# A state-space layer on one core: the output products set between the two key products, the finish behind the near levels, and a ring bank planned as read 2.4 steps on

## The chip, the core and the metric

The kernel runs on one core of a Trainium2 chip. The core's engines run side by side, each through its own list of instructions in order: TensorE multiplies matrices (its results go to a memory of their own, PSUM), VectorE and ScalarE work on tiles in SBUF and PSUM, GpSimd on tiles in SBUF, and it also issues the gathers; SyncE issues the other transfers. They wait for one another by semaphores. The metric is the device time of one execution in microseconds, lower is better.

## What is computed

Six layers of a small model on 4 sequences of 1024 positions of width 128: an expert layer, a state-space layer, the same expert layer again, then a layer of low-rank experts, an attention layer and the low-rank experts again. The change is in the state-space layer alone. Cut to what matters of it:

```python
proj = x @ W_in                       # z, x_raw, B (R=2 keys), C, dt, lam, theta
x_raw = silu(x_raw)
Bm = rms(Bm) * B_norm_bias;  Cm = rms(Cm) * C_norm_bias
dt = clip(softplus(dt_raw + dt_bias), 0.0001, 0.5)
ang = -cumsum(mean(dt) * theta)
Cr, Br = rope(Cm, cos, sin), rope(Bm, cos, sin)
xg = (lam * dt) * xh;  xb = ((1 - lam) * dt * alpha) * x_prev
cum = cumsum(log_dA) in each chunk of 128;  dmat = exp(cum_l - cum_m) for m <= l
y_intra = (C_l . B_m) * dmat * xg  +  (C_l . Bprev_m) * dmat * xb
S_next = exp(cum_end) * S + (decayed B, x of the chunk)
y_inter = C_l . S * exp(cum_l)
y = rms((y_intra + y_inter) * silu(z));  x = x + y @ W_out
```

## The kernel before

The layer (function `ssm`) is one stage of the program; the stages follow one another on all engines. The 4096 positions are 32 chunks of 128, numbered n, eight to a sequence (a "batch" b) and four to a group g. The heads' work is done for all 32 heads at once.

**One chunk**, in the order in which its data pass:

- TensorE transposes the rotated keys and queries of the chunk (`turn`, L1266, L1268) into a bank of the ring, and ScalarE copies them out to `bct` (`copy_turned`, L1472).
- TensorE multiplies keys with queries (`dots`, L1286 to L1289), once for each of the two keys r. Below these are called r0 and r1. Between them stands a wait for r0's result to be written. Blocks near the diagonal are masked on VectorE (`near_levels`, L1704, tile `near`), the far ones copied on ScalarE (`far_levels`, L1479).
- VectorE makes the weighted inputs `X` (`weigh`, L1713), GpSimd two more of them (L1539).
- TensorE forms the chunk's contribution to the state (`next_state`, L1297) and the output in three parts (`levels`: a first block of L1307, a second one of L1307, L1332 and L1335, and the product with the state, L1339). The blocks wait until VectorE has scaled those of the chunk before.
- VectorE carries the state on (`states`: the decay L1731 and the sum L1736) and scales and sums the three parts (`scale`, L1750, L1757, L1761, tile `ysum`).
- GpSimd multiplies with the gate (`sum_up`, L1549, tile `u_out`); ScalarE takes its squares (`square`, L1488); TensorE transposes it (`turn_out`, L1347), ScalarE copies that to `uT` (L1495).
- TensorE forms the output product (`project_out`, L1355), and VectorE adds it to the residual and takes the statistics for the next normalization (`finish`, L1768 and L108).

Three chunks are in flight in this manner, and between their instructions stands the preparation of later groups: projections (L1209, L1216, L1225), decays and rotations (`coefficients`, L1234 to L1254 on TensorE, L1597 to L1680 on VectorE), and the gathers of the expert layer's outputs (L263, added by VectorE in L271).

**The order** on each engine is written as step times. A helper (`interleave`) sorts all pieces on an engine by start plus step: `yield 21` in `project_out(n)` means "at K[n] + 21", where K[n] grows by 12 from chunk to chunk. Nothing runs at these times: they only give the order. So `dots(n+3)`, with steps -14 and -13, stands at K[n] + 22 and K[n] + 23.

**The ring** is four PSUM banks that all of TensorE's other results share, strictly in turn. A planner (`Uses`) gives each use its place in the turn, by the step at which it is written and the step by which it is planned to be read; where the bank would not be free by then it moves the whole rest of that stream to a later step. A stream wrapped in `moving(...)` follows its own moves. `dots`, `near_levels` and `far_levels` are not such streams: they stand at fixed steps.

Of the kernel before, what the change touches and what calls it, by code (L numbers as in the profile page):

```python
# [17 lines left out]
TILES = BATCHES * TIME // P  # L18
# [1059 lines left out]
def ssm(core, tag, weights, combine):  # L1078
# [14 lines left out]
    with ExitStack() as ctx:  # L1093
# [3 lines left out]
        def sem(name):  # L1097
            return core.stage_sem(f"{tag}_{name}")
# [48 lines left out]
        K = [FIRST + PERIOD * n for n in range(TILES)]  # L1147
# [8 lines left out]
        streams = {}  # L1156
# [6 lines left out]
        for n in range(TILES):  # L1163
            streams["t", n] = K[n], [(("t", n), -18, -16)]
            if n % NT < NT - 1:
                streams["st", n] = K[n], [(("st", n), -0.6, 2.6)]
            streams["u", n] = K[n], [(("u", n), 17.5, 19.5)]
            streams["r", n] = K[n], [(("r", n), 21, 23.5)]
        uses = Uses([ring[:, i, :] for i in range(4)], [sem(f"full{i}") for i in range(4)], [sem(f"free{i}") for i in range(4)], streams)

        def moving(name, stream):
            return 0, uses.moving(name, stream)
# [28 lines left out]
        with nc.Block(no_gpsimd_drain=True) as block:  # L1201
            @block.tensor
            def _(pe):
# [67 lines left out]

                def dots(n):

                    yield -14
                    uses.wait_read(pe, ("t", n))
                    if n:
                        pe.wait_ge(S["near_ready"], n)
                        pe.wait_ge(S["far_ready"], n)
                    for r in range(R):
                        if r:  # L1280
                            yield -13
                            pe.wait_ge(S["s_done"], 2 * n + 1)
                        rows, o = slice(r * N, (r + 1) * N), ps_s[:, n % 2, r, :]
                        k, q = bct[rows, n % 2, 0, :], bct[rows, n % 2, 1, :]
                        for m in range(0, P, BLOCK):
                            t_.matmul(o[m:m + 32, 0:32], k[:, m:m + 32], q[:, m:m + 32], start=True, stop=True, skip_group_check=True)  # L1286
                        for m in (0, 64):
                            t_.matmul(o[m:m + 32, 32:64], k[:, m:m + 32], q[:, m + 32:m + 64], start=True, stop=True, skip_group_check=True)
                        ins = t_.matmul(o[0:64, 64:128], k[:, 0:64], q[:, 64:128], start=True, stop=True, skip_group_check=True)  # L1289
                        ins.then_inc(S["s_done"], 1)  # L1290
# [57 lines left out]
                    uses.written(ins, ("u", n))  # L1348

                def project_out(n):  # L1350
                    yield 21
                    uses.wait_read(pe, ("u", n))
                    ps = uses.take(pe, ("r", n))
                    for i in range(2):
                        ins = t_.matmul(ps[:, 0:D], uT[:, n % 2, i, :], wout[:, i, :], start=(i == 0), stop=(i == 1))  # L1355
                    uses.written(ins, ("r", n))

                interleave([(K[n], levels(n)) for n in range(TILES)] + [(K[n], dots(n)) for n in range(TILES)] +
                           [moving(("t", n), turn(n)) for n in range(TILES)] + [moving(("st", n), next_state(n)) for n in range(TILES) if n % NT < NT - 1] +
                           [moving(("u", n), turn_out(n)) for n in range(TILES)] + [moving(("r", n), project_out(n)) for n in range(TILES)] +  # L1360
# [4 lines left out]
            def _(act):  # L1365
# [106 lines left out]
                    uses.read(s_.copy(bct[:, n % 2].rearrange("p j t -> p (j t)"), ps[:, 0:2 * P]), ("t", n))  # L1472

                def far_levels(n):
                    yield -10.8
                    act.wait_ge(S["near_ready"], n + 1)
                    if n >= 2:
                        act.wait_ge(S["o_done"], 3 * (n - 1))
                    s_.copy(far[0:96, n % 2], ps_s[0:96, n % 2, :, BLOCK:]).then_inc(S["far_ready"], 1)  # L1479
# [87 lines left out]
            def _(dve):  # L1567
# [128 lines left out]
                    rotate(1)  # L1696

                def near_levels(n):
                    yield -12
                    dve.wait_ge(S["s_done"], 2 * n + 2)  # L1700
                    if n >= 2:
                        dve.wait_ge(S["o_done"], 3 * (n - 1))
                    shape = [P, 4, R, BLOCK]
                    v.tensor_tensor(near[:, n % 2], ps_s[:, n % 2, :, 0:BLOCK].unsqueeze(1).broadcast_to(shape),  # L1704
                                    masks[:].unsqueeze(2).broadcast_to(shape), ALU.mult).then_inc(S["near_ready"], 1)
# [55 lines left out]
                    v.tensor_tensor(ysum[:], Y6[:, 0], Y6[:, 1], ALU.add).then_inc(S["summed_up"], 1)  # L1761

                def finish(n):
                    yield 23.5, ("r", n)
                    ps = uses.wait(dve, ("r", n))
                    dve.wait_ge(S["urs_ready"], n + 1)
                    xt = core.x[:, n, :]
                    uses.read(v.scalar_tensor_tensor(xt, ps[:, 0:D], urs[:, n % 2:n % 2 + 1], xt, ALU.mult, ALU.add), ("r", n))  # L1768
                    uses.wait_read(dve, ("r", n))
                    dve.sem_inc(S["added"], 1)  # L1770
                    core.count(n)
# [700 lines left out]
```

## Time and profile before

| what | value |
|---|---|
| median of 3 runs | 1458.83 us (1457.34 to 1461.06) |
| the profiled execution | 1452.51 us, span of its instructions 1450.7 us |
| mean granted clock of TensorE in it | 0.856 |
| TensorE busy (matmul) | 1167.0 us, 80% |
| VectorE busy | 1117.8 us, 77% |
| ScalarE busy | 804.8 us, 55% |
| GpSimd busy | 658.4 us, 45% |

Busy time is the time in which an engine worked on an instruction, including the time in which the instruction itself was held up. An idle time is put down to the instruction that ended it (the releaser). The granted clock is a share of full speed: 1.00 is 2.4 GHz and 0.50 is 1.2 GHz. In the rows of an order of time, neighbouring instructions of one kind are merged, with their count.

### The profile page before, as it was taken

What the parts mean: (1) busy time and instruction counts of PE and PEld (TensorE: products, weight loads), DVE (VectorE), ACT (ScalarE), POOL (GpSimd) and SP (SyncE); (2) the same over time, 40 slices, a digit from 0 to 9 for tenths busy, and PEclk for the clock granted to TensorE, in tenths of its full rate; (3) what the DMA queues carried; (4) which work ended last, traced back from release to release, by engine and by line L of the source; (5) the groups of instructions that cost most, each with busy time, mean ns of one, the idle gap of its engine ahead of it and who ended that gap; (6) DMA issues with size and microseconds to landing.
All of it is one profiled execution on the core that took longest, in us unless ns stands there. A gap on an engine that the chain in (4) does not pass through costs nothing. (4 is left out here: it accounts for less than half of the span.)

```text
span 1450.7 us, 32990 instructions
## 1 busy us (share of the span) xinstructions
PE 1167.0 (80%) x11380; PEld 740.1 (51%) x11380; DVE 1117.8 (77%) x2557; ACT 804.8 (55%) x1477; POOL 658.4 (45%) x859
## 2 busy tenths in 40 slices
PE   7679963798988989898848995458987988898894
PEld 6369952455545545554627994343433544443333
DVE  6959973888888897899786996567868877876644
ACT  3768844445235325311347884127876677778781
POOL 2366633763674674356347663453333431521100
PEclk6779985698988889999658997558998999999996
DMA  8035340000000000000502332000000000000000
GB/s 284 13 91 174 90 61 21 22 9 2 23 9 2 20 12 1 2 2 1 173 26 75 91 89 51 15 15 10 7 23 5 17 26 1 16 8 9 1 16 8
DMA packets 55714, 55.09 MB, mean 38 GB/s; under 512 B 9882, under 2 KB 44484, under 8 KB 55556
## 3 DMA queue, kind: packets, MB, share of 16 engines
q1 hardware_dynamic: 46468, 34.37, 7.5%
q0 software_dynamic: 9088, 18.63, 6.0%
q8 instruction: 98, 1.61, 0.5%
q14 instruction: 60, 0.49, 0.1%
HBM read 32.26 MB, written 20.71 MB: 37 GB/s over the span
## 5 line engine op out<-in xcount | busy, mean ns | idle before, releaser
L2143 ACT ACTIVATE l_probs<-l_ps 128x1024 f32<-128x1024 f32 (+1 forms) x320 | 288.0, 946 | 100.1 <-PE l_ps L2029 98.2
L781 POOL DMA_INDIRECT ffn_yg<-y_rows,ffn_index x156 | 156.1, 1001 | 82.5 <-PE ffn_ps_t L796 39.6
L2048 PE MATMUL l_ps<-l_probs,l_vs 128*32 128x512 f32 (+3 forms) x1536 | 165.1, 519 | 27.3 <-DVE l_oTs L2376 15.8
L864 ACT ACTIVATE ffn_hT<-ffn_ps_h,experts_b1T,experts_scales 128x256 f32<-128x256 f32 x312 | 151.1, 563 | 30.6 <-PE ffn_ps_h L811 29.8
L263 POOL DMA_INDIRECT combine_og<-o_rows,combine_place x128 | 139.3, 1088 | 54.0 <-issue 31.5
L1307 PE MATMUL ssm_ps<-ssm_X,ssm_near 32*32 32x256 f32 x2048 | 138.2, 421 | 1.9 <-DVE ssm_Y L1750 1.9
L2367 DVE TENSOR_TENSOR l_probs<-l_probs,last_tri 128x256 f32<-128x256 f32 x256 | 101.8, 435 | 41.4 <-ACT l_probs L2143 39.9
L2029 PE MATMUL l_ps<-l_qkT 32*128 32x512 f16 (+3 forms) x768 | 109.7, 338 | 18.1 <-ACT l_probs L2143 16.0
L889 DVE SCALAR_TENSOR_TENSOR ffn_h<-ffn_hT,experts_scales,ffn_h 128x512 f16<-128x512 f32 x156 | 117.2, 751 | 5.5
L827 PE MATMUL ffn_ps_o<-experts_w,ffn_h 128*128 x624 | 113.0, 220 | 2.1 <-DVE ffn_h L889 2.0
L1549 POOL TENSOR_TENSOR ssm_u_out<-ssm_ysum,ssm_zx 128x256 f32<-128x256 f32 x32 | 69.0, 2157 | 99.4 <-DVE ssm_ysum L1761 99.3
L829 PE MATMUL ffn_ps_o<-experts_w,ffn_h 128*128 x624 | 111.1, 220 | 0.0
L830 PE MATMUL ffn_ps_o<-experts_w,ffn_h 128*128 x624 | 111.1, 220 | 0.0
L886 DVE TENSOR_SCALAR ffn_h<-ffn_hT,experts_scales 128x512 f16<-128x512 f32 x156 | 80.9, 519 | 30.3 <-ACT ffn_hT L864 27.2
L2029 PEld LDWEIGHTS l_ps<-l_qkT 32*128 32x128 f16 x768 | 29.6, 92 | 145.8 <-ACT l_probs L2143 103.8
L1307 PEld LDWEIGHTS ssm_ps<-ssm_X,ssm_near 32*32 32x32 f32 x2048 | 66.0, 117 | 70.5 <-issue 38.2
L2214 POOL COPY l_vs<-l_V 128x144 f32<-128x144 f32 (+1 forms) x32 | 13.5, 421 | 181.6 <-PE l_ps L2048 181.5
L1750 DVE TENSOR_TENSOR ssm_Y<-ssm_ps,ssm_outp 128x512 f32<-128x512 f32 x96 | 65.1, 686 | 38.1 <-PE ssm_ps L1335 19.0
L1713 DVE TENSOR_TENSOR ssm_X<-ssm_zx,ssm_xw 128x2560 f32<-128x2560 f32 x32 | 90.3, 2821 | 0.1
L1479 ACT COPY ssm_far<-ssm_ps 96x192 f32<-96x192 f32 x32 | 10.1, 315 | 144.6 <-DVE ssm_near L1704 144.6
L809 PE MATMUL ffn_ps_h<-ffn_ygT,experts_w 128*128 128x256 f16 x312 | 86.8, 278 | 3.5 <-ACT ffn_ygT L855 3.4
L271 DVE SCALAR_TENSOR_TENSOR x_res<-combine_og,combine_gates,x_res 128x128 f32<-128x128 f32 x128 | 53.8, 420 | 44.2 <-DMA combine_og<-o_rows,combine_place 40.5
(354 smaller groups left out, 2965.9 us busy)
## 6 DMA issues: line engine op xcount, KB each, us to landing
o_rows<-ffn_out_sb SPq DMA_DIRECT2D x78, 128.0 KB, 1.9
y_rows<-ffn_y SPq DMA_DIRECT2D x8, 512.0 KB, 4.9
kept_w<-experts_w SPq DMA_DIRECT2D x16, 256.0 KB
experts_w<-kept_w SPq DMA_DIRECT2D x16, 256.0 KB, 5.6
ffn_yg<-y_rows,ffn_index POOLq DMA_INDIRECT x156
x_res<-in_L_attn_x SPq DMA_DIRECT2D x4, 512.0 KB, 6.2
prep_raw<-in_L_ffn_W SPq DMA_DIRECT2D x1, 2048.0 KB, 10.7
prep_raw<-in_L_ffn_W SPq DMA_DIRECT2D x8, 256.0 KB, 5.5
```

What stands on the lines that cost most here:

```text
L263: self.core.nc.gpsimd.indirect_dma_start(self.og[:, tile % GRING, k], None, self.o_rows.ap(), bass.IndirectOffsetOnAxis(ap=self.place[:, k ...
L781: g_.indirect_dma_start(yg[:, i % RING, j].rearrange("p n d -> p (n d)"), None, w.y_rows.ap(), bass.IndirectOffsetOnAxis(ap=index[:, n:n + ...
L827: t.matmul(o, h16[:, i % 2, 0, c, rows], high, start=(c == 0 and j == 0), stop=False, skip_group_check=True)
L829: t.matmul(o, h16[:, i % 2, 0, c, rows], low, start=False, stop=False, skip_group_check=True)
L830: ins = t.matmul(o, h16[:, i % 2, 1, c, rows], high, start=False, stop=(c == HC - 1), skip_group_check=True)
L864: s.activation(hT[:, i % 2, c, :], ps_h[:, i % 2, c, :], ACT.Gelu, bias=w.b1T[:, bass.ds(e * HC + c, 1)], scale=SC[:, 6:7]).then_inc(h_rea ...
L889: v.scalar_tensor_tensor(h16[:, i % 2, 1, part], hT[:, i % 2, part], SC[:, 5:6], h16[:, i % 2, 0, part], ALU.mult, ALU.subtract).then_inc( ...
L1307: ins = t_.matmul(o[rows], near[rows, n % 2, k, r, :], weighed(n, x, r, rows), start=start, stop=stop, skip_group_check=True)
L2029: ins = t_.matmul(ps_s[w % 2][:, i, at:at + width], qkT[r, b % 2, hg, 1, kb * P:(kb + 1) * P], qkT[r, b % 2, hg, 0, q0:q0 + width], start= ...
L2048: ins = t_.matmul(ps_o[VP * h:VP * h + VP, q0 % H:q0 % H + width], vs[:, s % 2, kb, h, :], probs[:, n % PSLOTS, i, at:at + width], start=( ...
L2143: s_.activation(probs[:, w % PSLOTS, i:i + n, 0:width], ps_s[w % 2][:, i:i + n, 0:width], ACT.Exp, scale=SCALE / (UNIT * UNIT)).then_inc(S ...
L2367: v.tensor_tensor(p, p, tri[:].unsqueeze(1).broadcast_to([P, n, P]), ALU.mult).then_inc(S["m_done"], 1)
```

## The change

Three numbers of steps are changed, and one list is added:

- `project_out(n)` stands at 22.6 instead of 21, that is between r0 (22) and r1 (23) of `dots(n+3)`.
- Its bank is planned as written at 22.6 and read at 25 (2.4 later), before at 21 and 23.5; `finish(n)` stands at 25 instead of 23.5, that is behind `near_levels(n+3)` (24) and the decay of chunk n+2 (24.5).
- `LATER[n]` is how far the planner has moved the transpose of chunk n, less 1.5. `dots`, `near_levels` and `far_levels` are put later by it. It is 1.6 for n = 6, 14 and 22, and 0 for all others.

```diff
-            streams["r", n] = K[n], [(("r", n), 21, 23.5)]
+            streams["r", n] = K[n], [(("r", n), 22.6, 25)]
         uses = Uses([ring[:, i, :] for i in range(4)], [sem(f"full{i}") for i in range(4)], [sem(f"free{i}") for i in range(4)], streams)
+
+        LATER = [max(0, uses.at(("t", n), -16) - (K[n] - 16) - 1.5) for n in range(TILES)]
...
                 def dots(n):
 
-                    yield -14
+                    yield -14 + LATER[n]
...
                         if r:
-                            yield -13
+                            yield -13 + LATER[n]
...
                 def project_out(n):
-                    yield 21
+                    yield 22.6
...
                 def far_levels(n):
-                    yield -10.8
+                    yield -10.8 + LATER[n]
...
                 def near_levels(n):
-                    yield -12
+                    yield -12 + LATER[n]
...
                 def finish(n):
-                    yield 23.5, ("r", n)
+                    yield 25, ("r", n)
```

Two lines are added, so all lines behind them are 2 higher in the changed kernel (L1731 is L1733 there).

On VectorE, in the last batch, the order of one chunk was

```order
L1761 TENSOR_TENSOR ssm_ysum<-ssm_Y 128x256
L1713 TENSOR_TENSOR ssm_X<-ssm_zx,ssm_xw 128x2560
L1768 SCALAR_TENSOR_TENSOR x_res<-ssm_ring,ssm_urs,x_res 128x128
L108 BN_STATS ln_stats<-x_res 128x6
L1704 TENSOR_TENSOR ssm_near<-ssm_ps,states_masks 128x256
L1731 TENSOR_TENSOR ssm_state<-ssm_state,ssm_outp 128x256
L1736 TENSOR_TENSOR ssm_state<-ssm_state,ssm_ring 128x256
L1750 TENSOR_TENSOR ssm_Y<-ssm_ps,ssm_outp 128x512 x2
```

and is in the changed kernel

```order
L1763 TENSOR_TENSOR ssm_ysum<-ssm_Y 128x256
L1715 TENSOR_TENSOR ssm_X<-ssm_zx,ssm_xw 128x2560
L1706 TENSOR_TENSOR ssm_near<-ssm_ps,states_masks 128x256
L1733 TENSOR_TENSOR ssm_state<-ssm_state,ssm_outp 128x256
L1770 SCALAR_TENSOR_TENSOR x_res<-ssm_ring,ssm_urs,x_res 128x128
L108 BN_STATS ln_stats<-x_res 128x6
L1738 TENSOR_TENSOR ssm_state<-ssm_state,ssm_ring 128x256
L1752 TENSOR_TENSOR ssm_Y<-ssm_ps,ssm_outp 128x512 x2
```

The finish and its statistics stand behind near and the decay. GpSimd's order does not change.

On TensorE, where the ring's plan is moved (chunk 6 in the stretch around 354 us), the order was

```order
L1355 MATMUL ssm_ring<-states_wout,ssm_uT 128x128 x2
L1266 MATMUL ssm_ring<-ident,ssm_rot 128x128
L1268 MATMUL ssm_ring<-ident,ssm_rot 64x128 x2
L1286 MATMUL ssm_ps<-ssm_bct 32x32 x4
L1288 MATMUL ssm_ps<-ssm_bct 32x32 x2
L1289 MATMUL ssm_ps<-ssm_bct 64x64
L1286 MATMUL ssm_ps<-ssm_bct 32x32 x4
L1288 MATMUL ssm_ps<-ssm_bct 32x32 x2
L1289 MATMUL ssm_ps<-ssm_bct 64x64
L1297 MATMUL ssm_ring<-ssm_X,ssm_rot 64x256 x2
L1307 MATMUL ssm_ps<-ssm_X,ssm_near 32x256 x28
```

and is

```order
L1268 MATMUL ssm_ring<-ident,ssm_rot 128x128
L1270 MATMUL ssm_ring<-ident,ssm_rot 64x128 x2
L1357 MATMUL ssm_ring<-states_wout,ssm_uT 128x128 x2
L1299 MATMUL ssm_ring<-ssm_X,ssm_rot 64x256 x2
L1288 MATMUL ssm_ps<-ssm_bct 32x32 x4
L1290 MATMUL ssm_ps<-ssm_bct 32x32 x2
L1291 MATMUL ssm_ps<-ssm_bct 64x64
L1309 MATMUL ssm_ps<-ssm_X,ssm_near 32x256 x24
L1288 MATMUL ssm_ps<-ssm_bct 32x32 x4
L1290 MATMUL ssm_ps<-ssm_bct 32x32 x2
L1291 MATMUL ssm_ps<-ssm_bct 64x64
L1309 MATMUL ssm_ps<-ssm_X,ssm_near 32x256 x4
```

The transpose of chunk 6 stands ahead of the output product of chunk 3 and takes its turn in the ring, r0 comes behind the state product of chunk 5, and r1 behind the first block of chunk 5's level products. VectorE's near of chunk 6 now stands behind its finish there, and ScalarE's far copy behind the scaling of twelve keys (L1437) and a square.

In the plain chunks TensorE's order changes from (output product, r0, r1) to (r0, output product, r1); in some of them a piece of the preparation stands between.

## Rows read from the trace of the kernel before

**Rows 1.** Busy time by stretch: length, PE, PEld, DVE, ACT, POOL, clock, DMA share, GB/s.

```profile
628.00:705.00 77.00, 65.51 (x824) 36.42 (x823) 66.97 (x93) 10.71 (x40) 41.20 (x34) 0.90 0.01 2
```

**Rows 2.** VectorE in order of time, last batch: start, duration, instruction, [idle before].

```profile
645.61 0.34 DVE L1768 SCALAR_TENSOR_TENSOR x_res<-ssm_ring,ssm_urs,x_res 128x128 f32<-128x128 f32 x1
...
646.30 0.41 DVE L1704 TENSOR_TENSOR ssm_near<-ssm_ps,states_masks 128x256 f32<-128x256 f32 x1
646.63 1.82 DVE L1731 TENSOR_TENSOR ssm_state<-ssm_state,ssm_outp 128x256 f32<-128x256 f32 x1
648.48 0.42 DVE L1736 TENSOR_TENSOR ssm_state<-ssm_state,ssm_ring 128x256 f32<-128x256 f32 x1
649.12 1.29 DVE L1750 TENSOR_TENSOR ssm_Y<-ssm_ps,ssm_outp 128x512 f32<-128x512 f32 x2 [0.21 <-DVE ssm_state L1736]
```

**Rows 3.** The decays on VectorE, last batch: count, ns shortest/median/longest, first and last start.

```profile
L1731 DVE TENSOR_TENSOR ssm_state<-ssm_state,ssm_outp x6: 1812/1815/1819, 636.7 to 686.5; 128x256 f32<-128x256 f32 x6
```

**Rows 4.** GpSimd in order of time, same chunk as rows 2.

```profile
643.03 3.24 POOL L1549 TENSOR_TENSOR ssm_u_out<-ssm_ysum,ssm_zx 128x256 f32<-128x256 f32 x1 [3.86 <-DVE ssm_ysum L1761]
646.23 1.93 POOL L1539 TENSOR_TENSOR ssm_X<-ssm_zx,ssm_xw 128x1024 f32<-128x1024 f32 x1
```

**Rows 5.** VectorE and GpSimd in order of time, near 296 us and 543 us.

```profile
296.29 0.99 DVE L1731 TENSOR_TENSOR ssm_state<-ssm_state,ssm_outp 128x256 f32<-128x256 f32 x1
...
296.88 0.97 POOL L1549 TENSOR_TENSOR ssm_u_out<-ssm_ysum,ssm_zx 128x256 f32<-128x256 f32 x1
...
543.00 0.41 DVE L1731 TENSOR_TENSOR ssm_state<-ssm_state,ssm_outp 128x256 f32<-128x256 f32 x1
...
542.33 0.73 POOL L1549 TENSOR_TENSOR ssm_u_out<-ssm_ysum,ssm_zx 128x256 f32<-128x256 f32 x1
543.01 2.20 POOL L1539 TENSOR_TENSOR ssm_X<-ssm_zx,ssm_xw 128x1024 f32<-128x1024 f32 x1
```

**Rows 6.** TensorE in order of time, same chunk; the last row is ScalarE.

```profile
646.33 0.44 PE L1347 MATMUL ssm_ring<-ident,ssm_u_out 128*128 128x128 f32 x2 [0.62 <-POOL ssm_u_out L1549]
...
647.78 0.71 PE L1355 MATMUL ssm_ring<-states_wout,ssm_uT 128*128 128x128 f32 x4 [0.54 <-ACT ssm_uT L1495]
648.42 0.27 PE L1286 MATMUL ssm_ps<-ssm_bct 64*32 64x32 f32 x8
...
649.06 0.27 PE L1286 MATMUL ssm_ps<-ssm_bct 64*32 64x32 f32 x8
...
649.56 0.65 PE L1297 MATMUL ssm_ring<-ssm_X,ssm_rot 128*64 128x256 f32 x4
...
647.63 0.37 ACT L1472 COPY ssm_bct<-ssm_ring 128x256 f32<-128x256 f32 x1
```

**Rows 7.** TensorE in order of time, around 354 us; the last two rows are VectorE.

```profile
353.75 0.68 PE L1355 MATMUL ssm_ring<-states_wout,ssm_uT 128*128 128x128 f32 x4 [3.16 <-DVE ssm_xw L1641]
...
355.39 0.33 PE L1286 MATMUL ssm_ps<-ssm_bct 64*32 64x32 f32 x8 [0.47 <-ACT ssm_bct L1472]
...
358.09 4.36 PE L1307 MATMUL ssm_ps<-ssm_X,ssm_near 32*32 32x256 f32 x44
362.09 0.40 PE L1332 MATMUL ssm_ps<-ssm_X,ssm_far 32*32 32x256 f32 x2
...
359.79 0.41 DVE L1736 TENSOR_TENSOR ssm_state<-ssm_state,ssm_ring 128x256 f32<-128x256 f32 x1
...
363.52 0.69 DVE L1750 TENSOR_TENSOR ssm_Y<-ssm_ps,ssm_outp 128x512 f32<-128x512 f32 x1
```

**Rows 8.** VectorE in order of time, the chunk after rows 7.

```profile
372.84 0.42 DVE L1704 TENSOR_TENSOR ssm_near<-ssm_ps,states_masks 128x256 f32<-128x256 f32 x1 [1.21 <-PE ssm_ps L1289]
...
376.18 0.69 DVE L1750 TENSOR_TENSOR ssm_Y<-ssm_ps,ssm_outp 128x512 f32<-128x512 f32 x1 [2.12 <-PE ssm_ps L1307]
```

**Rows 9.** TensorE's idle time before line 1286, whole stage: releaser, us, times.

```profile
  PE ssm_ps L1289: 5.0, 23
```

**Rows 10.** As rows 1, for three microseconds of the last batch.

```profile
660.00:663.00 3.00, 3.00 (x24) 1.13 (x28) 2.90 (x6) 0.00 (x0) 0.05 (x1) 0.50 0.03 5
```

## The prediction

> **What bounds the kernel now.** I read the page first: the changed code is one stage, the state-space layer, which runs from about 281 to 705 us. The next stage starts only when this one is over on all engines, so what the stage loses or gains goes to the end at full size. Then the busy time by stretch [rows 1]: in the last part of the stage, 628 to 705 us, no engine is full: TensorE is busy 65.5 of 77 us, VectorE 67.0, at a mean granted clock of 0.90. So the bound changes from place to place, and must be read from the order of time. Two places matter.
>
> In the last batch (chunks 25 to 30) VectorE has no idle time but the 0.21 us behind its own state sum [rows 2]. The decays of the state, one per chunk, start from 636.7 to 686.5 us [rows 3]: five periods in 49.8 us, 9.96 us each. VectorE sets that pace. TensorE waits twice in a period, 0.62 us for GpSimd's u_out and 0.54 us for the copy uT [rows 6], so it needs 9.96 - 0.62 - 0.54 = 8.80 us.
>
> Elsewhere in the stage TensorE is mostly ahead of VectorE in the queue for time: VectorE stands 1.21 us for the key products and 2.12 us for the first level products of the chunk [rows 8]. There a reordering on VectorE costs or gives nothing, and one on TensorE counts.
>
> **The change, part by part.**
>
> *Finish behind near levels and decay, on VectorE (all chunks).* No instruction is added. The decay (L1731) has two inputs in SBUF. In the last batch it takes 1.81 us, six times of six [rows 3]; at 543 us, with nothing in front of it, 0.41 us [rows 5]. What it waits for is GpSimd: the product L1539 starts at 646.23 and runs 1.93 us, to 648.16, and the decay that started at 646.63 ends at 648.45 [rows 2, 4], 0.29 us after it. Now follow the new order from 645.61, where the finish started and near can start: near has its input long before (its products were done a chunk ago) and takes 0.33 us from start to next start, so the decay is ready at 645.94. GpSimd is then still in u_out, which ends at 643.03 + 3.24 = 646.27 [rows 4]. The decay waits 0.33 us for that, runs 0.42 us, and is over at about 646.7. Finish and its statistics take 646.30 - 645.61 = 0.69 us [rows 2], so the state sum starts at about 647.4 instead of 648.48: 1.07 us saved per chunk. Six chunks give 6.4 us.
>
> That needs the decay to get in between two GpSimd instructions that stand behind one another. Rows speak for it: the decay of 296.29 took 0.99 us, so it ended at 297.28, and the u_out that started at 296.88 took 0.97 us instead of 0.73 [rows 5]; and at 543.00 the decay took its 0.41 us where u_out ended at 543.06, and L1539, started at 543.01, took 2.20 us instead of 1.93. In both the waiting decay went first and GpSimd's next instruction paid about 0.25 us. L1539 is then 0.4 us later in each chunk; it is used a chunk later, and GpSimd's share is low (41 of 77 us, rows 1), so this costs nothing. The Trainium skill, "SBUF — State Buffer", section "Who interferes with whom", says that a VectorE instruction with two SBUF inputs and a GpSimd instruction that reads SBUF exclude each other for the whole instruction, and that the order of issue decides. The trace agrees (1.81 against 0.41 us). The page does not say who is next when one waits and the other has a second instruction behind; by it alone the gain could be 0 or 1.07 us a chunk.
>
> How much of the 6.4 us TensorE lets through: the new VectorE period is 9.96 - 1.07 = 8.9 us, TensorE's need 8.80, so the gain just fits. I take off 0.4 us for the six chunks together, since TensorE's order changes too (next part). Last batch: -6.0 us.
>
> *Output product between the two key products, on TensorE.* Before: wait for uT, output product, products r0, a wait of 0.2 us for r0 to be written, r1. After: wait for bct, r0, output product, r1. The short wait is filled: 5.0 us in 23 places over the stage [rows 9]. Against it, where TensorE stands idle for uT, the output product used to run while ScalarE made bct (uT released it at 647.78, bct was ready at 647.63 + 0.37 = 648.0 [rows 6]); now TensorE stands until 648.0. From 648.0: r0 0.44, output product 0.64, r1 about 0.5, so the next state product at 649.6 against 649.56. Nothing gained where it waits for uT. But uT itself stands on ScalarE behind the far copy, which waits for near, and near is 0.69 us earlier: in the last batch that makes bct about 0.3 us earlier, which is what holds TensorE's need at 8.8. Where TensorE is the bound and does not wait for uT, the 0.2 us is real; I count four such chunks, -0.8 us. Bounds: 0 and -5.0 us (all of rows 9).
>
> In the other chunks with a wait for key products on VectorE, near starts no earlier, and finish, once in that wait, now comes after: the state sum is 0.69 us later. VectorE then stands 2.12 us for TensorE anyway [rows 8], which hides it: 0 (bounds 0 and +0.7 in each of six such chunks).
>
> *Shifted ring plan (chunks 6, 14, 22).* The transpose of these chunks moves ahead of the output product of the chunk three back, the state product ahead of r0, and r1 behind the first 24 level products. From 353.75 to 362.09 TensorE needs 8.34 us, of which 0.47 us is a wait for bct [rows 7] and about 0.15, rounded down from rows 9, the wait for r0. Both are filled: the second block of level products, at 362.09, starts 0.6 us earlier, three times: -1.8 us. Price on VectorE: near now waits for r1, which ends just before that second block, at about 361.5. Behind it stand near itself (0.33) and, from the state sum to the first scaling, 363.52 - 359.79 = 3.73 us [rows 7]: the first scaling comes at 365.5, 2.0 us later. In the next chunk VectorE has 1.21 + 2.12 us of idle time [rows 8], so it is hidden. Bounds per place: -1.1 and +2.0 us.
>
> Sum: -6.0 - 0.8 - 1.8 = **-8.6 us**. The profiled execution took 1452.51 us (span 1450.7), so its like after the change would take 1443.9. It lies 6.3 us under the median of the runs shown, 1458.83; on the median the same sum gives **1450.2 us**.
>
> **The rivals.**
>
> *GpSimd keeps the port (slower).* If L1539, issued right at the end of u_out, takes the port before the waiting decay, the decay ends at 648.45 as before and finish with its statistics comes behind it: +0.69 us in each of six chunks, +4.1 us. It decides at one point: whether the decay, ready 0.33 us before u_out ends, goes first. With the other two terms at nothing this gives 1463.0; with them 1460.4. For it: L1539 seems to start (646.23) even before u_out's end. Against it: both cases of rows 5.
>
> *TensorE takes over.* The need of 8.80 us holds at the full clock. In the last batch there are 3 us and more at half the clock [rows 10]; if it stays so, TensorE, not VectorE, is late after each such stretch, and half of the 6.4 us is lost: about -5, 1453.8 us. Such a stretch follows idle time of TensorE, of which there would be less.
>
> *The clock helps too.* If that stretch goes away because of less waiting, TensorE gets about 3 us back and other waits for uT shrink as near comes earlier: 1445.
>
> *The shifted places cost.* If the 2.0 us on VectorE is not hidden in three places, +6.0 instead of -1.8: 1458.0.
>
> *Nothing moves.* If the decay still lands in L1539 because all engines shift together: 1458.
>
> **How the numbers follow.** Forecast 0.50 (own range 1447 to 1453); clock helps 0.08; TensorE takes over 0.14, half of it beyond 0.3%; shifted places 0.10; port kept 0.12, of which 0.10 slower than 0.3%, as other decays would be held too; nothing 0.06. 0.3% is 4.4 us, about what a measurement of this kernel can tell from no change. Faster: 0.50 + 0.08 + 0.08 = 0.66; same: 0.06 + 0.10 + 0.02 + 0.06 = 0.24; slower 0.10. Range: 1445 to 1460, which leaves out most of the port case and the best end.
>
> **What would show it.** Right: in the last batch the decays take 0.75 us or so instead of 1.81, L1539 takes over 2 us, and their starts are 8.9 us apart. Wrong: decays still at 1.8 us with the statistics behind them, or TensorE without waits there. In the shifted chunks VectorE should stand about 1.7 us before near, and the next level products should come 0.6 us earlier. What would make the prediction wrong as a whole: half-clock stretches at other places, each worth 2 to 3 us of TensorE's time.

## The result: 0.8% faster, and the profile after

| what | before | changed |
|---|---|---|
| median, 4 runs each | 1459.38 us (1457.34 to 1461.06) | 1445.15 us (1442.62 to 1452.10) |
| the profiled execution | 1452.51 us | 1452.10 us |
| its span | 1450.7 us | 1450.3 us |
| mean granted clock | 0.856 | 0.860 |
| next stage begins at | 705.10 us | 698.45 us |

The ratio is 0.9918, 95% interval 0.9897 to 0.9940: 12 us less by the ratio and 14.2 by the two medians, where 8.6 were forecast. The two profiled executions look equal, and that is chance: that of before lies 5 us under the lowest of its other runs, that of the changed kernel is the highest of its four. Inside the trace the gain is plain until well into the last stage. VectorE in order of time (start, duration, instruction, idle before), changed kernel, first row the beginning of the next stage, second row an addition in the attention layer:

```profile
698.45 0.21 DVE L119 TENSOR_TENSOR ln_tmp<-ln_stats 128x32 f32<-128x32 f32 x1 [0.39 <-PEq L1203]
...
1143.67 0.68 DVE L2397 SCALAR_TENSOR_TENSOR x_res<-l_ps,x_res 128x512 f32<-128x512 f32 x1
```

and of before:

```profile
705.10 0.21 DVE L119 TENSOR_TENSOR ln_tmp<-ln_stats 128x32 f32<-128x32 f32 x1 [0.39 <-PEq L1201]
...
1150.22 0.68 DVE L2395 SCALAR_TENSOR_TENSOR x_res<-l_ps,x_res 128x512 f32<-128x512 f32 x1
```

6.65 us ahead at the stage's end, 6.55 still at 1144 us. Then it is lost, in code that the change doesn't touch, and the last column but two (granted clock) says where. Busy time by stretch (length, PE, PEld, DVE, ACT, POOL, clock, DMA share, GB/s), changed kernel:

```profile
1144.00:1228.00 84.00, 74.69 (x614) 36.52 (x615) 64.96 (x185) 58.69 (x76) 23.39 (x47) 0.92 0.05 14
...
1266.00:1343.00 77.00, 70.43 (x575) 31.99 (x576) 53.34 (x143) 58.01 (x73) 13.51 (x31) 0.89 0.03 8
```

and the same pieces of work before:

```profile
1150.00:1231.00 81.00, 71.02 (x608) 34.20 (x608) 64.74 (x185) 58.71 (x76) 23.92 (x48) 0.96 0.05 14
...
1270.00:1343.00 73.00, 66.70 (x590) 30.32 (x592) 53.24 (x143) 58.84 (x74) 12.97 (x30) 0.98 0.03 9
```

In the first pair the changed kernel needs 84 us at a clock of 0.92 for what took 81 at 0.96. At 1266 us it is 3.4 us ahead, at 1343 it is 1.2 us behind. It is the trace of before that is unusual: what comes behind the state-space stage takes 745.6 us in it, and 750.1 to 757.2 us in the nine other traces of the table below. A second profile of the same kernel (`after_again`, below) ended its stage at 691.37 us and its span at 1441.8. So one pair of profiles can't give the total here; the medians do, and the traces tell the mechanism within the stage.

**The last batch** did what was forecast. VectorE and GpSimd in order of time, changed kernel, to be held against [rows 2, 4]:

```profile
664.37 0.42 DVE L1706 TENSOR_TENSOR ssm_near<-ssm_ps,states_masks 128x256 f32<-128x256 f32 x1
664.70 0.61 DVE L1733 TENSOR_TENSOR ssm_state<-ssm_state,ssm_outp 128x256 f32<-128x256 f32 x1
665.35 0.35 DVE L1770 SCALAR_TENSOR_TENSOR x_res<-ssm_ring,ssm_urs,x_res 128x128 f32<-128x128 f32 x1
665.85 0.29 DVE L108 BATCH_NORM_STATS2 ln_stats<-x_res 128x6 f32<-128x128 f32 x1
666.06 0.40 DVE L1738 TENSOR_TENSOR ssm_state<-ssm_state,ssm_ring 128x256 f32<-128x256 f32 x1
...
661.79 3.24 POOL L1551 TENSOR_TENSOR ssm_u_out<-ssm_ysum,ssm_zx 128x256 f32<-128x256 f32 x1 [2.55 <-DVE ssm_ysum L1763]
665.00 2.11 POOL L1541 TENSOR_TENSOR ssm_X<-ssm_zx,ssm_xw 128x1024 f32<-128x1024 f32 x1
```

The decay is ready at 664.70, waits for u_out's end (661.79 + 3.24 = 665.03), runs, and is over at 665.31. GpSimd's product behind it takes 2.11 us, 0.18 more than before: it paid the wait. From near's start to the state sum VectorE needs 1.69 us; before it needed 648.48 - 645.61 = 2.87 us for the same four instructions [rows 2]. The decays as a group (count, ns shortest/median/longest, first and last start), as in [rows 3]:

```profile
L1733 DVE TENSOR_TENSOR ssm_state<-ssm_state,ssm_outp x6: 614/619/621, 637.4 to 682.2; 128x256 f32<-128x256 f32 x6
```

The last four periods are 8.77 us (the first 9.77, with a half-clock stretch from 631 to 638 us just ahead of it), where all were 9.96. VectorE still sets the pace: it has no idle time but the 0.22 us behind its state sum. The half-clock stretch that before has from 659 us on is gone, as one rival had it, but it is not what gives the gain: before's periods are 9.96 with it and without it.

**TensorE's waits** in the stage moved. The product's and the key products' groups, changed kernel (busy us, mean ns | idle us ahead, by releaser):

```profile
L1357 PE MATMUL ssm_ring<-states_wout,ssm_uT 128*128 128x128 f32 x128 | 24.0, 314 | 1.4 <-ACT ssm_uT L1497 1.4
...
L1288 PE MATMUL ssm_ps<-ssm_bct 64*32 64x32 f32 x480 | 16.4, 208 | 14.1 <-ACT ssm_bct L1474 14.1
```

before:

```profile
L1355 PE MATMUL ssm_ring<-states_wout,ssm_uT 128*128 128x128 f32 x128 | 24.2, 317 | 26.6 <-ACT ssm_uT L1495 17.2 <-DVE ssm_xw L1641 9.5
...
L1286 PE MATMUL ssm_ps<-ssm_bct 64*32 64x32 f32 x480 | 17.0, 215 | 2.7 <-ACT ssm_bct L1472 1.4
```

The 5.0 us between r0 and r1 [rows 9] are gone, and the wait for uT (17.2 us) has become one for bct (14.1 us); with the 1.4 us of the other kind on each side it is 23.6 us before and 15.5 after. Other waits of TensorE in the stage grew meanwhile: those for the layer's input y (`ssm_y`), for the state and for the scaling together take 22.4 us where they took 14.8. Whether the move is worth anything the experiments have to say.

**A shifted place**, chunk 6. TensorE and VectorE in order of time, changed kernel, to be held against [rows 7]:

```profile
355.98 0.30 PE L1268 MATMUL ssm_ring<-ident,ssm_rot 128*128 128x128 f32 x1 [3.16 <-DVE ssm_xw L1643]
...
357.81 0.27 PE L1288 MATMUL ssm_ps<-ssm_bct 64*32 64x32 f32 x8
...
358.46 4.24 PE L1309 MATMUL ssm_ps<-ssm_X,ssm_near 32*32 32x256 f32 x48
362.63 0.26 PE L1288 MATMUL ssm_ps<-ssm_bct 64*32 64x32 f32 x8
...
363.25 0.42 DVE L1706 TENSOR_TENSOR ssm_near<-ssm_ps,states_masks 128x256 f32<-128x256 f32 x1 [1.48 <-PE ssm_ps L1291]
```

No wait for bct is left, near stands 1.48 us for r1 (I had said 1.7), and from the end of the wait to the second block TensorE takes 7.19 us where it took 8.34: 1.15 less, not 0.6. In the two other places it takes 7.10 and 7.07.

### The profile page after: what moved, and what is told of

It reads as the page before. It is cut to its first block and busy times, and to the rows that moved or that the text cites. A ratio compares the mean times of both kernels' runs of the same rounds, so it can differ in the third digit from the quotient of the medians.

```text
span 1450.3 us, 32972 instructions
## 1 busy us (share of the span) xinstructions
PE 1165.1 (80%) x11380; PEld 740.9 (51%) x11380; DVE 1116.0 (77%) x2557; ACT 806.5 (56%) x1477; POOL 660.2 (46%) x859
## 5 line engine op out<-in xcount | busy, mean ns | idle before, releaser
L263 POOL DMA_INDIRECT combine_og<-o_rows,combine_place x128 | 143.8, 1124 | 54.8 <-issue 32.9
L1309 PE MATMUL ssm_ps<-ssm_X,ssm_near 32*32 32x256 f32 x2048 | 132.3, 406 | 4.6 <-DVE ssm_Y L1752 4.6
L809 PE MATMUL ffn_ps_h<-ffn_ygT,experts_w 128*128 128x256 f16 x312 | 86.9, 279 | 3.4 <-ACT ffn_ygT L855 3.3
L811 PE MATMUL ffn_ps_h<-ffn_ygT,experts_w 128*128 128x256 f16 x312 | 86.9, 279 | 0.0
L810 PE MATMUL ffn_ps_h<-ffn_ygT,experts_w 128*128 128x256 f16 x312 | 86.9, 279 | 0.0
```

What stands on the lines that cost most here:

```text
L263: self.core.nc.gpsimd.indirect_dma_start(self.og[:, tile % GRING, k], None, self.o_rows.ap(), bass.IndirectOffsetOnAxis(ap=self.place[:, k ...
L1309: ins = t_.matmul(o[rows], near[rows, n % 2, k, r, :], weighed(n, x, r, rows), start=start, stop=stop, skip_group_check=True)
```

## The experiments

Each kernel is compared with runs of the kernel before on the same chip, in between its own. For the stage itself I use one number from each trace, its length from the first near (chunk 0) to the beginning of the next stage, and three parts of it:

| kernel | what it has of the change | ratio to before (95%) | stage, us | the three places, us | last batch, five sums, us |
|---|---|---|---|---|---|
| before | nothing | | 429.1 | 8.34, 8.52, 8.26 | 50.15 |
| finish_alone | finish | 0.9990 (0.9969 to 1.0011) | 424.7 | 8.41, 8.51, 8.53 | 43.86 |
| product_alone | output product | 1.0067 (1.0047 to 1.0088) | 434.6 | 8.61, 8.73, 8.72 | 50.15 |
| shift_alone | shift | 0.9995 (0.9974 to 1.0016) | 423.3 | 6.79, 6.83, 6.83 | 50.16 |
| no_product | finish, shift | 0.9886 (0.9858 to 0.9914) | 414.0 | 6.79, 6.79, 6.79 | 43.84 |
| no_finish | product, shift | 0.9972 (0.9951 to 0.9992) | 423.4 | 7.05, 7.04, 7.04 | 50.15 |
| no_shift | finish, product | 0.9973 (0.9954 to 0.9993) | 421.5 | 8.29, 8.68, 8.73 | 43.86 |
| changed, first profile | all | 0.9918 (0.9897 to 0.9940) | 422.5 | 7.19, 7.10, 7.07 | 43.85 |
| after_again | all | 0.9924 (0.9901 to 0.9948) | 416.1 | 7.05, 7.04, 7.04 | 43.84 |
| decay_first | decay moved, no part of the change | 0.9956 (0.9932 to 0.9979) | 424.1 | 8.21, 8.57, 8.50 | 45.45 |

"Places" is the time from the end of TensorE's wait for xw (3.15 or 3.16 us in every one) to the start of its second block of level products, for chunks 6, 14 and 22. "Five sums" is the time between the starts of the tile ysum of chunks 25 and 30, read from the order of time. The stage column holds one execution each; the changed kernel's two differ by 6.4 us, so it is a guide and no verdict. The last two columns repeat to 0.02 us and, but for the clock (below), to 0.1 to 0.3 us.

### One part at a time

`finish_alone`, against the changed kernel:

```diff
-        LATER = [max(0, uses.at(("t", n), -16) - (K[n] - 16) - 1.5) for n in range(TILES)]
+        LATER = [0 for n in range(TILES)]
-            streams["r", n] = K[n], [(("r", n), 22.6, 25)]
+            streams["r", n] = K[n], [(("r", n), 21, 25)]
-                    yield 22.6
+                    yield 21
```

> Only the finish is moved behind the near levels and the decay (step 25); the output product stays at 21 and nothing is shifted. Port theory: GpSimd's second product of X no longer holds the decay, so in the last batch the decays take about 0.62 us (1.81 before) and start 8.8 us apart (9.96 before): about -7 us between the decays of chunks 25 and 30, all of the change's gain there. In the part of the stage before 628 us the finish ahead of the state sum costs what it costs in the changed kernel, 0 to +1 us. Total about 1450. Rival (the order on TensorE is what made it possible): the starts stay over 9.4 us apart, because TensorE then waits for uT in front of the key products, and less than half of the gain comes.

The decays took 615 to 620 ns, and the five sums 43.86 us where before has 50.15: the whole gain of the last batch, with TensorE's order as it was. The rival (TensorE's order makes it possible) falls. The ratio of 0.9990 is no measurable gain in the total, although the stage is 4.4 us shorter in its trace.

`product_alone`: the same with 22.6 kept, its bank planned as read at 23.5, and `finish` back at 23.5.

> Only the output product is moved between the two key products (step 22.6); the finish stays at 23.5 ahead of near, nothing is shifted. Port theory: the decays of the last batch stay at 1.81 us and 9.96 us apart, nothing is gained there; in the chunks before, 0 to -0.8 us from the filled wait between r0 and r1. Total within 2 us of before. Rival (TensorE's order carries the gain): the last batch's starts come under 9.5 us apart.

Its decays stay at 1.82 us and the five sums at 50.15, as the port theory says. But it is slower than before by 0.67%, which neither theory had. Its trace shows a wait of VectorE's finish that was 1.0 us in 3 times before (us, times, longest):

```profile
DVE x_res L1770 <- PE ssm_ring L1357: 7.6, 8, 1.9
```

and, behind the batch boundaries, additions of the gathered rows held by GpSimd, VectorE then GpSimd near 414 us:

```profile
414.50 3.42 DVE L271 SCALAR_TENSOR_TENSOR x_res<-combine_og,combine_gates,x_res 128x128 f32<-128x128 f32 x2
...
415.45 1.93 POOL L1541 TENSOR_TENSOR ssm_X<-ssm_zx,ssm_xw 128x1024 f32<-128x1024 f32 x1
```

Such a pair takes 0.73 us when it is free. In this trace pairs near 297, 384, 414, 503 and 533 us are held; before has those near 297, 384 and 500. Of the stage's 5.5 us more in this trace, 3.0 come between the sums of chunks 8 and 9, at 414 us; that the held pair there costs nothing, and the clock does, is shown under `after_again`. What the other 2.5 us and the rest of the 0.67% come from isn't shown.

`shift_alone`: `LATER` as in the changed kernel, all other numbers as before.

> Only the list of shifts is added (key products, near and far copy of chunks 6, 14 and 22 are 1.6 steps later). My prediction: second block of level products 0.6 us earlier at three places, -1.8 us up to 628 us, last batch as before (9.96 us apart). Rival (it costs VectorE 2 us per place, not hidden): up to +6 us by 628 us.

The places take 6.8 us in place of 8.3 to 8.5, 1.4 to 1.7 less in each; between the tile ysum of chunks 4 and 7, 12 and 15, 20 and 23 the stage is 1.7, 2.0 and 1.8 us shorter. So the sign and the hiding on VectorE were right and the size was three times too small. The total shows nothing (0.9995).

`after_again` is the changed kernel.

> The changed kernel again, for the spread. If the state-space stage runs alike in every execution, its end lies again at 698.4 us, within 0.5 us, and the executions' differences (1442.6 to 1452.1 us) come from the attention layer, behind 1100 us. Rival: the stage's end itself wanders by some microseconds with the half-clock stretches.

The rival is right: the stage ended at 691.37 us, 7.1 us earlier than in the first profile. Of that 0.6 us lie ahead of the stage, 1.4 us come in chunk 1, where only the first profile has a half-clock stretch (290 to 293 us), 1.0 us in chunks 4 and 5, and 3.3 us between the sums of chunks 8 and 9. At this last step a pair is held as in product_alone. First profile, VectorE, GpSimd and TensorE:

```profile
415.72 3.04 DVE L271 SCALAR_TENSOR_TENSOR x_res<-combine_og,combine_gates,x_res 128x128 f32<-128x128 f32 x1
...
416.67 1.93 POOL L1541 TENSOR_TENSOR ssm_X<-ssm_zx,ssm_xw 128x1024 f32<-128x1024 f32 x1
...
417.13 3.92 PE L1309 MATMUL ssm_ps<-ssm_X,ssm_near 32*32 32x256 f32 x48
```

`after_again`, the same additions:

```profile
411.60 0.74 DVE L271 SCALAR_TENSOR_TENSOR x_res<-combine_og,combine_gates,x_res 128x128 f32<-128x128 f32 x2
```

In the one it was ready 0.3 us before GpSimd's u_out and was held through that and the product of X; in the other it was over before u_out began. Whether it meets them differs from execution to execution. But the hold is not what costs the 3.3 us. In decay_first (below) the same addition is held even longer, and its sum of chunk 9 comes 0.4 us later than in before, as that of chunk 8 does:

```profile
414.81 3.17 DVE L271 SCALAR_TENSOR_TENSOR x_res<-combine_og,combine_gates,x_res 128x128 f32<-128x128 f32 x1
...
414.68 2.79 PE L1307 MATMUL ssm_ps<-ssm_X,ssm_near 32*32 32x256 f32 x48
```

What differs is the clock. The first profile and product_alone have half clock from 402 to 419 us, decay_first only to 412.3, and `after_again` to 409. The first block of level products takes 3.92 and 4.35 us in the first two, 2.79 in the others, and VectorE then waits for TensorE. So the two executions of the changed kernel differ here by the clock.

### One part taken away

`no_product`, against the changed kernel (the output product back at 21, ahead of both key products):

```diff
-            streams["r", n] = K[n], [(("r", n), 22.6, 25)]
+            streams["r", n] = K[n], [(("r", n), 21, 25)]
-                    yield 22.6
+                    yield 21
```

> The changed kernel with the output product back ahead of both key products (step 21, planned read at 25). If the parts only added up (finish alone -3.0, shift alone -2.7 us in the medians so far) it would take 1452 us. If the output product's move is worth something once the finish stands behind near, it is slower than the changed kernel's 1445 by 3 us or more, with TensorE waiting for uT again (some 8 to 12 us in the stage) ahead of the key products. In the last batch 8.8 us between decays by either.

1443.25 us against 1460.88, ratio 0.9886: not slower than the changed kernel (0.9924), the opposite of what a useful move would give. TensorE does wait for uT again, 8.3 us in 8 places, and it costs nothing. At the places it takes 6.79 us, 0.25 less than with the product between (7.04 and 7.05 in `after_again`, with the same half clock).

`no_finish`: finish back at 23.5, product and shift kept.

> The changed kernel with the finish back ahead of near (step 23.5). Theory of the tie: VectorE's finish then waits for an output product that now stands behind r0 (7.6 us of such waits when the product was moved alone), and near, the decay and the gathers' additions come later and fall into GpSimd's product of X. Expected 1460 to 1465 us, that is 15 to 20 us above the changed kernel; last batch 9.96 us between decays. If the parts only added up: 1464. If the shift is what saves the product's move: 1455.

1455.95 us: 11 us above the changed kernel's median, 7 us by the two ratios, less than the 15 to 20 expected. Five sums 50.15. Its stage, 423.4 us, is that of shift_alone; with the shift the product's move does not do the harm that it did alone.

`no_shift`: `LATER` zero, the rest kept.

> The changed kernel with the list of shifts at zero. Its three places then have 6.8 us of half clock near 355, 471 and 584 us again (3.4 with the shift) and each is 1.8 us longer: 3 x 1.8 = 5.4 us above the changed kernel, 1450 to 1451. By my prediction's own term it would be 1.8 us above it, 1447. The gathers' additions near 384 and 500 us are held by GpSimd again (2.76 us for the pair, 0.73 without).

1455.54 us, ratio 0.9973: 10 us above the changed kernel by the medians and 7 us by the ratios, where my term gives 1.8 and the places' 1.8 us each 5.4. Places of 8.29 to 8.73 us, and the pairs of L271 near 385 and 501 us held for 2.75 and 2.76 us as before.

So the finish and the shift each carry some 7 to 10 us of the total when the other one is there, and little that can be measured alone. The sum of the three medians alone is +4 us (-3.0, +9.6, -2.7), all together -12.7. I can't say from one profile each what ties them; the totals also hold the attention layer, whose clock wanders by 3 us or more.

The traces show where part of it lies. Counted from the first near, the sum of chunk 24 comes 5.0 to 5.5 us earlier than in before in four of the five traces with the shift (1.4 us later in the changed kernel's first profile), and 2.8 to 6.6 us later in the four without it. From there to the stage's end the five traces with the finish moved gain 7.9 to 10.7 us and decay_first 7.9; the three others gain 0.4 to 1.1. So the trace of before itself runs better through the middle of the stage than the other four without the shift: they lose 2.7 to 2.9 us against it between the sums of chunks 15 and 22, and all four have 10.2 us of half clock from 518 to 522 us on, where before has 6.8. Whether its other executions do so too isn't known. The half clock in the stage sums to 104.9 us in before, 84.6 and 81.6 in the changed kernel's two traces and 76.0 in no_product, so a part of the gain in the stage is the clock.

### The port

`decay_first`, against the kernel before:

```diff
-                        yield 0.5
+                        yield -1
```

> The kernel before with one edit: the decay stands at step -1 in place of 0.5, right behind VectorE's X and ahead of the finish and near. Port theory: it then waits for GpSimd's u_out alone (0.66 us) and runs ahead of its second product of X: about 1.07 us in place of 1.81 in the last batch. VectorE's own sequence gets 0.75 us shorter per chunk, but near comes 0.4 to 1.1 us later in it than before, and with it the far copy, the square and uT: the starts are 9.2 us apart if TensorE lets it through, up to 9.96 if uT then holds it. Rival (GpSimd keeps the port, its next instruction being queued): the decay takes over 2.4 us and the starts are 10.5 us apart.

```profile
665.45 0.95 DVE L1731 TENSOR_TENSOR ssm_state<-ssm_state,ssm_outp 128x256 f32<-128x256 f32 x1
...
662.87 3.24 POOL L1549 TENSOR_TENSOR ssm_u_out<-ssm_ysum,ssm_zx 128x256 f32<-128x256 f32 x1 [2.76 <-DVE ssm_ysum L1761]
666.07 2.11 POOL L1539 TENSOR_TENSOR ssm_X<-ssm_zx,ssm_xw 128x1024 f32<-128x1024 f32 x1
```

The decay is ready at 665.45, u_out ends at 666.11, and the decay is over at 666.40; it took 0.95 us in all six chunks, and GpSimd's product again 2.11. The rival, 2.4 us and more, falls. The starts are 9.08 us apart (6 starts from 638.2 to 683.6 us), a little better than expected, and the total is 0.44% under before, without any part of the change. This one edit shows the mechanism by itself: it is a matter of being in line ahead of GpSimd's long product. In the last batch the changed kernel's order is better still, since near, which needs no wait, fills part of the time; the total doesn't say so (0.9956 here, 0.9990 for finish_alone, on two chips).

That the waiting VectorE instruction goes first holds for these decays, and not always. In the trace of before, right behind the decay of 296.29 [rows 5], VectorE and GpSimd:

```profile
297.31 2.97 DVE L271 SCALAR_TENSOR_TENSOR x_res<-combine_og,combine_gates,x_res 128x128 f32<-128x128 f32 x2
...
296.88 0.97 POOL L1549 TENSOR_TENSOR ssm_u_out<-ssm_ysum,ssm_zx 128x256 f32<-128x256 f32 x1
297.82 1.92 POOL L1539 TENSOR_TENSOR ssm_X<-ssm_zx,ssm_xw 128x1024 f32<-128x1024 f32 x1
```

This addition was ready 0.5 us before u_out ended, and was still held through the product of X behind it: the first of the two took 2.58 us, alike in all ten traces. Near 384 us another addition, ready 0.66 us before the end of u_out, went first and took 0.82 us. What decides between them no run shows.

### The clock at the shifted places

Read microsecond by microsecond, the granted clock in the ten traces of the table shows 6.8 us of half clock at all 15 places of the five without the shift, and 3.4 us at all 15 of the five with it. Why the shifted order brings the full clock back sooner isn't shown. One trace more held the control that I could not have built.

`no_product_again`, the kernel of no_product on another chip:

> The changed kernel without the move of the output product, again, beside the changed kernel on the same chip. By the first comparison it takes 1443 us and the changed kernel 1445: the move of the output product is worth nothing, or costs 1 to 2 us. By my prediction's term for it (-0.8) it should be 0.8 us slower than the changed kernel.

Its first two places take 6.79 and 6.78 us, its third 8.44 us, the same kernel and the same instructions. TensorE, second and third place:

```profile
486.61 0.68 PE L1357 MATMUL ssm_ring<-states_wout,ssm_uT 128*128 128x128 f32 x4 [3.15 <-DVE ssm_xw L1643]
489.56 3.37 PE L1309 MATMUL ssm_ps<-ssm_X,ssm_near 32*32 32x256 f32 x48
...
599.33 0.68 PE L1357 MATMUL ssm_ring<-states_wout,ssm_uT 128*128 128x128 f32 x4 [3.16 <-DVE ssm_xw L1643]
602.29 5.01 PE L1309 MATMUL ssm_ps<-ssm_X,ssm_near 32*32 32x256 f32 x48
```

and the clock behind each (columns as in the first such fence):

```profile
487.00:493.00 6.00, 6.00 (x86) 3.09 (x84) 5.15 (x7) 3.65 (x16) 0.97 (x3) 0.72 0.00 0
600.00:606.00 6.00, 6.00 (x60) 3.03 (x62) 4.88 (x7) 3.64 (x15) 0.74 (x2) 0.50 0.02 5
```

With 6.8 us of half clock the shifted place takes 8.44 us, as long as an unshifted one (8.3 to 8.5); with 3.4 us it takes 6.79. So the shift's gain at the places is the clock, 1.65 us, and the order by itself gives about nothing.

`fill_before` asks it the other way round: the kernel before, with TensorE kept at work through its idle 3.16 us.

```diff
                     yield 21
+                    if n in (3, 11, 19):
+                        for _ in range(13):
+                            t_.matmul(ps_s[:, (n + 3) % 2, 0, :], core.ident[:], core.ident[:], start=True, stop=True,
+                                      skip_group_check=True)
                     uses.wait_read(pe, ("u", n))
```

> The kernel before with 13 extra matmuls of the identity (128 x 128, into the free half of the key products' bank, results unused) in TensorE's idle time of 3.16 us near 350, 466 and 579 us, ahead of the output product of chunks 3, 11 and 19. Clock theory: the half-clock stretches of 6.8 us that follow those idle times vanish or shrink to 3.4 us, and the stretch from that output product to the second block of level products (8.53 us in the trace of before, 7.26 with the shift) falls to about 6.9 to 7.3; 1.2 to 1.6 us won per place inside the stage, with no shift of the key products. Rival (the shift's gain was the order, the clock followed it): the half-clock stretch stays as it is, nothing is won.

TensorE at the first place (the trace counts each of these matmuls twice), and the clock at all three, in stretches of 6 us that begin 0.3 to 0.5 us behind the output product's start:

```profile
367.37 3.07 PE L1354 MATMUL ssm_ps<-ident 128*128 128x128 f32 x26
370.70 0.68 PE L1359 MATMUL ssm_ring<-states_wout,ssm_uT 128*128 128x128 f32 x4 [0.26 <-DVE ssm_xw L1645]
...
376.26 0.40 PE L1332 MATMUL ssm_ps<-ssm_X,ssm_far 32*32 32x256 f32 x2
```

```profile
371.00:377.00 6.00, 5.47 (x105) 3.29 (x107) 5.75 (x9) 2.01 (x9) 0.00 (x0) 1.00 0.01 3
487.00:493.00 6.00, 5.47 (x107) 3.19 (x109) 5.67 (x9) 2.13 (x9) 0.00 (x0) 1.00 0.01 3
603.00:609.00 6.00, 5.47 (x107) 3.19 (x109) 5.66 (x9) 2.15 (x9) 0.00 (x0) 1.00 0.02 5
```

Full clock throughout, and 5.56 us where before takes 8.3 to 8.5: 2.8 us less, with not one useful instruction moved. The rival falls. Before was not traced on this chip; the changed kernel was, and its places took 7.05, 7.16 and 7.04 us there, as on the first chips. The total is 0.61% under before (0.9915 to 0.9963).

`fill_best` is no_product with the same matmuls.

> The changed kernel without the move of the output product (as in no_product), with the same extra matmuls. Clock theory: the 3.4 us of half clock left at the three places goes too, up to 1.2 us each, so 1440 to 1443 us against 1443 to 1444; VectorE stands between the two at these places, which may take part of it. Rival: unchanged, or up to 1 us slower because the extra matmuls run over the idle time.

The places take 5.40 us, against 5.56 with the order of before: at equal, full clock the shift's order is worth 0.16 us, not 0.6. The median went the wrong way, though: 1493.08 us against 1484.62 for no_product_again on the same chip, ratios of 0.9904 (0.9871 to 0.9936) and 0.9850 (0.9816 to 0.9883), which just overlap. Its trace has half clock elsewhere: 17.1 us from 534 us on, where no_product_again has 6.8, and in the whole stage 81.9 us against 78.7. That filling is of use on top of the shift is not shown.

`after_third`:

> The changed kernel on the same chip as the three runs before it: 1442 to 1447 us in the median, 12 us under the kernel before.

This chip was slower for every kernel (before took 1509.23 us in the median), so only the ratios among these four kernels count: changed 0.9893 (0.9855 to 0.9931), no_product 0.9850 (0.9816 to 0.9883). The medians say the same as on the first chip, 7.5 us for leaving the output product where it was, but the intervals overlap. It has the lowest ratio of all versions, on both chips where it ran; that it beats the changed one is likely and not settled.

## Why the prediction was right, step by step

- **GpSimd keeps the port, or the decay goes first** (the point on which the main term stood). The decay goes first in all 6 chunks of every kernel that has it there. Forecast 0.75 us a decay, measured 0.62; periods forecast 8.9 us, measured 8.77. The term was -6.0 us; from 0.70 us behind at chunk 25's near to 6.65 us ahead at the stage's end it was -7.4 in the first profile. The allowance of 0.4 us for TensorE wasn't needed, and the rival in which TensorE takes over did not come: VectorE sets the pace at 8.77 too. The rule of the Trainium skill, "SBUF — State Buffer", "Who interferes with whom", holds: GpSimd and a two-input VectorE instruction exclude each other for the whole instruction. Its measure here is the decay of 1.81 us against 0.41. The decays, waiting, went ahead of the product that GpSimd had next, as the prediction took it from [rows 5]. As a rule that is too wide: the addition right behind the first of those rows was held through GpSimd's next product too (2.58 us). Two rows in favour were read, and the one against, 0.03 us further on, was not.
- **The output product between the key products**, -0.8 us. The wait between r0 and r1 did go, all 5.0 us of it. The step that failed is that a filled wait of TensorE counted at four chunks: no experiment shows a gain from the move, alone it costs 0.67%, and without it the kernel is as fast or faster. At the places it costs 0.25 us.
- **The shifted places**, -1.8 us in three. The mechanism was wrong. I priced the filled waits at 0.6 us a place; at equal clock the order gives 0.16 or nothing. What comes with the shift is half as long a half-clock stretch behind TensorE's 3.16 us of idle time (20 of 21 places), 1.65 us a place, and that is worth 1.7 to 2.0 us from the sum ahead of a place to the one behind. The 2.0 us on VectorE was hidden, as forecast: chunk 5's sum comes 0.7 to 1.1 us late, chunk 6's no longer.
- **Nothing from finish behind near elsewhere**: finish_alone is at +0.3 us at chunks 0 and 7 against before, so the term of 0 holds in the first batch; later in that trace it falls back by 3.2 us by chunk 23, beside longer half-clock stretches (10.2 us from 519 us on, before 6.8), and I can't part the two. The three other traces without the shift fall back at the same place, decay_first among them, which leaves the finish where it was.
- **The sum** came out at -8.6 for -12 because the first and third terms were too small by 1.4 and some 3 to 4 us, as far as single traces can say. The range of 1445 to 1460 held it by 0.15 us (median 1445.15), the narrower 1447 to 1453 did not, and 1445 is the number of the rival "the clock helps too". That rival had the place wrong (the last batch, where VectorE sets the pace) and the kind right: the largest error of the sum is the clock at the shifted places. The mechanism of the main term was right; that the total still landed in the range with the third one wrong is partly luck.

## What to carry to other kernels

When a short VectorE instruction with two inputs in SBUF takes four times its time, look at what GpSimd runs beside it, and try to move it a place or two so that it stands in line ahead of GpSimd's long instruction instead of behind it; then read in the trace whether it does go first. Price a wait of TensorE not only by its length but by the half-clock stretch that stands behind it in the rows: at one place here 3.16 us of idle time was followed by 2.8 us of lost time. And where executions differ by a few microseconds in stages that the change doesn't touch, judge a mechanism by the length of its own stretch of work, and the total by medians.

## What the runs showed of the hardware

- A VectorE instruction with two inputs in SBUF that waits for GpSimd can go ahead of GpSimd's next instruction: decays of 0.62 us (behind near) and 0.95 us (alone) against 1.81, with GpSimd's next product 2.11 us in place of 1.93. It doesn't always: an addition ready 0.5 us before the end of one GpSimd instruction was held through the next as well (2.58 us).
- Pairs of additions of gathered rows beside GpSimd's work took 2.75 to 3.55 us in place of 0.73, at places that change from execution to execution; where such a hold could be compared (chunk 9), it cost the chunk nothing.
- The half-clock stretch behind the same idle time of 3.16 us was 6.8 us or 3.4 us; with TensorE at work through it there was none, and the place took 8.2 to 8.7, 6.8 to 7.2 or 5.4 to 5.6 us accordingly. The same kernel showed both of the first two on one chip.
- The changed kernel's stage took 422.5 us and 416.1 us in two executions on work that is the same; half of that lies in one chunk, where 48 level products took 3.92 us at half clock and 2.79 at full clock.
